# Gated cross-attention block with an FP8 feed-forward on one core: the output products of the feed-forward trail by five steps at the end

## What is computed

```
x = x + tanh(g_xattn) * _L0_xattn_ref(_layernorm(x), ctx, Wq, bq, Wk, bk)
#   query = ctx @ Wq.T + bq; key = ctx @ Wk.T + bk
#   attention = softmax(query @ key.T); result = x_normalised @ attention.T (over the 256 features)
x = x + tanh(g_ffn) * _L0_ffn_ref(_layernorm(x), w_gating, w_linear)
#   gate = gelu(q(x) @ q(w_gating[0])); up = q(x) @ q(w_gating[1])      256 -> 1024
#   outputs = q(gate * up) @ q(w_linear)                                1024 -> 256
#   q(...) rounds to float8 e4m3
```

## Time and profile before

| | |
|---|---|
| median of 3 runs | 50.71 us (50.47 to 51.29) |
| the profiled execution | 50.6 us |
| its span, first to last instruction | 48.8 us |
| TensorE busy | 42.2 us (87%) |
| VectorE busy | 35.7 us (73%) |
| ScalarE busy | 29.4 us (60%) |
| GpSimd busy | 16.9 us (35%) |

### The profile page before, as it was taken

One profiled execution on the slowest core, in us unless ns is written; L12 is line 12 of the kernel. 1 busy time (PEld: TensorE's weight loads), 2 busy tenths in 40 slices (PEclk: granted clock), 3 DMA queues, 4 the chain that ended last, 5 costly groups with the idle time before them and its releaser, 6 DMA issues.

```text
span 48.8 us, 842 instructions
## 1 busy us (share of the span) xinstructions
PE 42.2 (87%) x245; PEld 29.2 (60%) x245; DVE 35.7 (73%) x111; ACT 29.4 (60%) x67; POOL 16.9 (35%) x35
## 2 busy tenths in 40 slices
PE   0989999990999999998999999999999999995300
PEld 0318788860887988864435655766656788872000
DVE  2101059999978979989999991887666998899910
ACT  4601684399799599844599749754446944662000
POOL 3205992009999823410510160000000697005000
PEclk9999999999999999999999999999999999999965
DMA  0599999999999990000000000000000024400083
GB/s 0 81 320 153 336 378 309 186 203 196 199 199 139 105 95 4 0 0 7 0 13 0 0 0 0 0 0 0 7 0 0 0 104 164 168 8 0 0 322 108
DMA packets 3460, 4.64 MB, mean 95 GB/s; under 512 B 384, under 2 KB 2048, under 8 KB 3456
## 3 DMA queue, kind: packets, MB, share of 16 engines
q1 hardware_dynamic: 2592, 3.80, 24.6%
q0 software_dynamic: 864, 0.79, 17.3%
HBM read 5.90 MB, written 1.05 MB: 142 GB/s over the span
## 4 chain that ended last, share of the span: by engine, by line
PE 64%; DVE 15%; DMA 9%; SPq 3%; ACT 2%; issue 1%; DVEq 1%
PE bank L627 15%; PE bank L633 14%; PE bank L652 14%; PE bank L587 14%; DMA x_sb<-x 9%; DVE st L403 6%; PE bank L559 4%; SPq L206 3%; DVE nmax L410 2%; PE bank L609 2%; PE bank L552 2%; DVE mv L406 2%; DVE aq L470 2%; DVE attn L421 1%; ACT xq L337 1%
## 5 line engine op out<-in xcount | busy, mean ns | idle before, releaser
L461 DVE SCALAR_TENSOR_TENSOR ap<-bank,gl 128x512 f16<-128x512 f32 (+1 forms) x20 | 11.6, 581 | 3.5 <-issue 1.6
L346 ACT ACTIVATE gl<-bank 128x512 bf16<-128x512 f32 (+1 forms) x20 | 10.0, 508 | 6.0 <-PE bank L627 6.0
L652 PE MATMUL bank<-wl,aq 128*128 128x256 fp8e4 x64 | 10.1, 273 | 0.7 <-DVE aq L470 0.6
L627 PE MATMUL bank<-xq,wg 128*128 128x512 fp8e4 (+1 forms) x40 | 10.2, 337 | 0.2 <-ACT xq L337 0.2
L633 PE MATMUL bank<-xq,wg 128*128 128x512 fp8e4 (+1 forms) x40 | 10.2, 337 | 0.0
L652 PEld LDWEIGHTS bank<-wl,aq 128*128 128x128 f16 x64 | 6.0, 98 | 4.1 <-DVE aq L470 1.6
L587 PE MATMUL bank<-attnT,xT_sb 128*128 128x256 f32 x32 | 8.1, 385 | 0.0
L470 DVE TENSOR_SCALAR aq<-ap 128x512 uint16<-128x512 uint16 (+1 forms) x20 | 6.6, 334 | 0.0
L276 POOL TENSOR_TENSOR yo<-ys,x 128x256 f32<-128x256 f32 x4 | 2.9, 748 | 9.3 <-ACT ys L354 9.3
L587 PEld LDWEIGHTS bank<-attnT,xT_sb 128*128 128x128 f32 x32 | 5.6, 190 | 0.7 <-ACT attnT L320 0.2
L261 POOL TENSOR_TENSOR r<-ve,neg_half 128x2 f32<-128x2 f32 x4 | 3.0, 760 | 8.4 <-DVE ve L444 8.4
(11 more groups left out here) (51 smaller groups left out, 55.7 us busy)
## 6 DMA issues: line engine op xcount, KB each, us to landing
x_sb<-x SPq DMA_DIRECT2D x4, 256.0 KB, 4.8
xT_sb<-xT SPq DMA_DIRECT2D x4, 256.0 KB, 8.4
out<-yo SPq DMA_DIRECT2D x6, 128.0 KB, 2.0
wg<-w_gating POOLq DMA_DIRECT2D x4, 128.0 KB, 9.1
par<-params_ctxT SPq DMA_DIRECT2D x1, 258.0 KB, 2.8
par<-params_ctxT SPq DMA_DIRECT2D x1, 256.0 KB, 4.0
wl<-w_linear POOLq DMA_DIRECT2D x2, 128.0 KB, 11.7
out<-yo SPq DMA_DIRECT2D x1, 256.0 KB, 2.0
```

Source lines behind the costliest of these rows:

```text
L346: nc.scalar.activation(gl[:, s % 2, toks], gate_b[s % 2][:, toks], ACT.Gelu_apprx_tanh).then_inc(gelu_ready, 1)
L461: nc.vector.scalar_tensor_tensor(ap[:, s % NAP, toks], up_b[s % 2][:, toks], ACT_SCALE, gl[:, s % 2, toks], ALU.mult, ALU.mult).then_inc(p ...
L627: mm = nc.tensor.matmul(gate_b[s % 2][:, toks], wg8[:, c, k, 0, o:o + P], xq[:, g, k, toks], start=(k == 0), stop=(k == KC - 1))
L652: mm = nc.tensor.matmul(halves(y_b[g][i])[:, t], aq[:, s % NAQ, m:m + P], wl8[:, j], start=(j == 0 and t == 0), stop=(j == HT - 1), skip_g ...
```

## The change

It has four parts. The output products of a step follow a table instead of a fixed lag: three steps back up to step 9, none behind steps 10 and 11, five steps back from step 12 on, and the last five steps' behind everything. There are eight buffers `aq` instead of five. ScalarE's scalings of batches 0 and 1 stand behind gelu 13 and 14 instead of 11 and 12. GpSimd's last addition waits for the last rounding as well as for its scaling.

```diff
-    NAQ = 5
-    LAG = 3
+    NAQ = 8
...
+    FFN2_AT = {s: (s - 3,) for s in range(3, 10)}
+    FFN2_AT |= {s: (s - 5,) for s in range(12, S)}
+    OUT_AT = (HT + 5, HT + 6)
...
             pool.wait_ge(scaled_ready, GB + 1)
+            pool.wait_ge(aq_ready, S)
             nc.gpsimd.tensor_tensor(yo[:, 2, 1], ys[:, 2, 1], x2[:, 2, 1], ALU.add).then_inc(pool_y_ready, 1)
...
-                if s == HT + LAG:
+                if s == OUT_AT[0]:
                     scale_out(0)
-                if s == HT + LAG + 1:
+                if s == OUT_AT[1]:
                     scale_out(1)
...
                 ffn1(s)
-                if s >= LAG:
-                    ffn2(s - LAG)
+                for done in FFN2_AT.get(s, ()):
+                    ffn2(done)
...
-            for s in range(S - LAG, S):
+            for s in range(S - 5, S):
                 ffn2(s)
```

## The result

The change made the kernel faster by one per cent: 50.30 us against 50.86 (medians of 20 runs each), ratio 0.990, interval 0.987 to 0.993. The ratio leaves out the few executions that lay over 1.5% above the fastest of their kernel, so it is not quite the quotient of the medians. Forecast were 49.9 us and 0.71 us off. By the ratio 0.52 us are off, between 0.36 and 0.68. The time lies within the range of 49.4 to 50.4 us, and the change stays within two per cent, to which the prediction gave 0.75.

What follows compares the result with a forecast made beforehand. TensorE was taken to bound the feed-forward steps, then a latency chain, and the in-order store queue the end. Stores 0.76 us sooner less 0.05 for transfers gave 0.71 off 50.60: 49.9 us, range 49.4 to 50.4.

Steps and rivals of the forecast that it cites:

- rival 2: Additions beside later steps delay VectorE, up products stall: 0.1 to 0.45 us given back, 50.0 to 50.3 us; chance 0.12.
- TensorE's head start: Step 19's gate product comes 0.55 us sooner: 0.65 from moved output products and a lost stall, less 0.10 for a wait.
- The stall at step 10's output products: Step 10's output products, now behind step 15, wait no more for their rounding; the 0.21 us stall goes.
- the one at step 12's up product: New TensorE wait for step 10's product on VectorE, bounded by 0.06 and 0.20 us, taken as 0.10.
- The weight load: At step 12's up product: if the weight load goes late as well, the wait costs 0.20 us.
- Step 13's: Step 13's up product, due about 38.0, finds its product ended about 37.9: covered by 0.05 to 0.1 us.
- The last rounding: Step 19's rounding on VectorE, no addition beside it, takes 0.22 us and ends at 44.14 for 45.17, 1.04 us sooner.
- Scaling and addition: ScalarE's last scaling waits for TensorE until 43.64; GpSimd's last addition starts 44.19, ends 44.91; its new wait costs nothing or 0.05.
- The stores: Three final stores leave one queue in order, first 44.93, last 45.80: 0.76 us sooner, transfers adding 0.05.
- Rival 1: The stores' queue does not bind, the last finishing operation on VectorE does: 1.04 us gained, 49.56 us; chance 0.20.
- Rival 3: Finishing operations hold off GpSimd's last addition; last store leaves 0.55 us later than before, 51.15 us; chance 0.04.

Runs made afterwards that it cites:

- e8: The changed kernel with the output products that stand behind step 12 put between its gate and up product; ratio to before 0.988 (0.982 to 0.994).
- e3: The changed kernel without GpSimd's wait for the last rounding; ratio to before 0.986 (0.982 to 0.989), 14.70 us behind step 10 for 14.79.
- e4: The changed kernel with batch 2's store issued from ScalarE's queue instead of SP's; ratio to before 0.986, 14.87 us behind step 10 for 14.79.
- e5: The changed kernel with batch 3's two 128 KB stores made one of 256 KB; ratio to before 0.989, 14.71 us behind step 10 for 14.79.
- e6: The changed kernel with batch 2's store split into two halves, the first sent once VectorE has it; ratio to before 0.991, 14.82 us behind step 10.
- e12: The changed kernel storing only the half of batch 2 from GpSimd's addition, leaving the other out; ratio to before 0.988, 14.71 us behind step 10.
- e7: The changed kernel with five buffers for rounded products instead of eight; ratio to before 0.991 (0.987 to 0.995), 14.79 us behind step 10.
- e11: The changed kernel with ScalarE's scalings of batches 0 and 1 one gelu earlier; ratio to before 0.984 (0.977 to 0.991), 14.78 us behind step 10.

## Why the prediction came out right, step by step

- *The number.* The 49.9 us was counted from the profiled execution of before, 50.60 us, and the median of 20 runs before is 50.86; 0.71 off that would be 50.15, for 50.30 measured. The 0.52 us off by the ratio and 0.58 by the profile lie at the lower edge of what the forecast was given (0.55 to 0.95), and rival 2, with 0.10 to 0.45 of the 0.71 given back, would have left 0.26 to 0.61. The time alone does not tell the two apart; the profile does, below.
- *TensorE's head start.* Predicted 0.55 us for step 19's gate product, measured 8.05 - 7.54 = 0.51. The stall at step 10's output products went, the one at step 12's up product came, and cost 0.13 us where I took 0.10. The weight load did wait for the product, the case that I had bounded by 0.20 without a row. Step 13's was covered, as said, by very little: e8 shows that it is next.
- *The last rounding.* Predicted to end 1.04 us sooner at 0.22 us. It took 0.23 and ended at 44.34; counted from step 10 that is 8.95 us for 45.17 - 35.23 = 9.94, so 0.99.
- *Scaling and addition.* The scaling waits for TensorE, as worked out, and starts 8.45 us behind step 10's gate product, predicted 8.41. The addition was to start at 8.96 and started at 44.48 - 35.39 = 9.09. This is the mis-sized term: of the 0.13 us that it was late, 0.04 are the scaling's, and 0.09 are the new wait, which I had priced at nothing or 0.05. e3 measures it, 0.09 to 0.10.
- *The stores.* The last was to leave 0.87 us after the first, and left 0.85 after it; in all 10.70 us behind step 10, predicted 10.57. That is 0.63 us sooner than before, where 0.76 were predicted, and the last one landed 0.05 us later behind its issue than before, as predicted: 0.58 for 0.71. (Half a megabyte is 524,288 bytes, so 1.39 us at 378 GB/s and not 1.35; the engines were busy with it for 1.47 us.)
- *Why that term held* is another matter. I called the queue of stores the bound, with the transfers as a correction of at most 0.1 us. They are a bound of their own, equally tight (e4 and e5). The sum came out because the two limits coincided; that was luck. The advice that it implied, relieve the queue, would have failed.
- *Rival 1* (the last finishing operation binds, 1.04 us) is out: the last store left 0.39 us behind it, and making it leave at once gave nothing. *Rival 2* (the additions hurt in their new place): they stretched two roundings, to 0.69 and 0.43 us (lines below), and from step 14 on nothing on TensorE waited for VectorE but the last output products, for their own rounding. *Rival 3* (addition against finishing operations): the first two of these ran beside the addition from 44.48 to 45.21, at 0.48 us each, as before, and the addition took 0.73. The rule of the Trainium skill cited there ("SBUF — State Buffer", "Who interferes with whom") holds in this trace: a VectorE operation with one tensor in PSUM and one in SBUF did not contend with GpSimd.

The two roundings beside the four additions, after:

```profile
40.94 0.69 DVE L474 TENSOR_SCALAR aq<-ap 128x256 uint16<-128x256 uint16 x1
...
41.88 0.43 DVE L474 TENSOR_SCALAR aq<-ap 128x256 uint16<-128x256 uint16 x1
```

## What to carry to other kernels

Matmuls that nobody waits for soon belong behind the last link of the latency chain at the end, not ahead of it; the length of the trail is found by asking which step's product and rounding can still be late without being missed. Where a bound at the end is named, the next one should be priced as well: here the issue queue and the full transfer engines lay some 0.1 us or less apart, and relieving one of them looked like proof that neither mattered. And a wait that keeps two engines apart is only worth having while they would meet.

## What the runs showed of the hardware

- The 16 transfer engines were full (share 0.97 to 1.03) while storing half a megabyte at the end, at 328 to 389 GB/s; stores of 128 KB issued by one queue every 0.37 to 0.49 us (e6 and e12) kept them only 76 to 80% busy.
- Half a megabyte in packets of 2 KB (e5) took the 16 engines 1.35 us of busy time, half of it in packets of 1 KB (after) 1.47, all of it in packets of 1 KB (e6) 1.54.
- An issue on SP's queue took 0.33 us in one place and 0.42 to 0.45 in another, for transfers of the same size; the two stores of batch 3 differ in this between before (0.33, 0.43) and after (0.43, 0.45). What sets it, no run here tells.
- The load of `x`, with nothing changed around it, took 4.29 to 5.20 us in eleven of the profiles, and moved what is behind it. The profiled executions of after, e7 and e11 took 50.18, 49.84 and 49.49 us and had the same 14.78 to 14.79 behind step 10: what they differ by lies ahead of it.
